# GpSimd takes two of the four normalisations of each step in the second node stage of a graph network

## The reference

```python
def _layernorm(x, axis=-1, eps=1e-05):
    m = jnp.mean(x, axis=axis, keepdims=True)
    v = jnp.var(x, axis=axis, keepdims=True)
    return (x - m) / jnp.sqrt(v + eps)
...
    x = _layernorm(x + _L0_gnn_ref(x, edge_index, L0_gnn_W1, L0_gnn_b1, L0_gnn_W2, L0_gnn_b2), axis=-1)
    x = _layernorm(x + _L1_gnn_ref(x, node_vec1, src, dst, edge_attr_4, ...), axis=-1)
```

## Time and profile before

| | |
|---|---|
| time, median of 3 executions | 7610.92 us (7610.32 to 7613.86) |
| the profiled execution, its own time | 7614.77 us |
| its span in the trace | 7612.9 us |
| mean granted clock of TensorE | 0.872 of full speed |
| busy share of the span: PE, VectorE, ACT, GpSimd | 87%, 62%, 45%, 64% |
| second node stage: first load issued to the edge stage's first load issued | 3411.7 to 3529.1 us from the span's start |
| edge stage, from then on | 4083 us |

### The profile page before, as it was taken

One profiled execution on the slowest core, in us unless ns is written; L12 is line 12 of the kernel. 1 busy time (PEld: TensorE's weight loads), 2 busy tenths in 40 slices (PEclk: granted clock), 3 DMA queues, 4 the chain that ended last, 5 costly groups with the idle time before them and its releaser, 6 DMA issues.

```text
span 7612.9 us, 125645 instructions
## 1 busy us (share of the span) xinstructions
PE 6617.5 (87%) x37688; PEld 5566.4 (73%) x37689; DVE 4748.7 (62%) x9176; ACT 3399.5 (45%) x6948; POOL 4890.6 (64%) x4864
## 2 busy tenths in 40 slices
PE   6899987999987999986888888888888888888887
PEld 4666656888876888875777777777777777777776
DVE  9999984333334333337666666666666666666665
ACT  5999974555545555543222222222222222222322
POOL 2211103777774777774777777777777777777775
PEclk9999999999999999998777777777777778787876
DMA  3666556555545555544223333233233333333331
GB/s 81 131 133 131 125 121 188 162 167 167 166 136 167 166 167 167 167 140 138 83 85 85 84 84 85 84 85 85 84 85 84 84 85 84 84 85 84 85 84 55
DMA packets 604288, 868.26 MB, mean 114 GB/s; under 512 B 217478, under 2 KB 470461, under 8 KB 599025
## 3 DMA queue, kind: packets, MB, share of 16 engines
q0 software_dynamic: 158000, 437.63, 22.0%
q1 hardware_dynamic: 419980, 414.21, 19.2%
q10 hardware_dynamic: 26036, 12.80, 0.6%
HBM read 706.91 MB, written 157.30 MB: 114 GB/s over the span
## 4 chain that ended last, share of the span: by engine, by line
POOL 34%; issue 13%; DMA 3%; DVE 2%; POOLq 1%; DVEq 0%; SPq 0%; PE 0%; ACT 0%; ACTq 0%
POOL t_rows L1758 34%; DMA t_rows<-table,t_ends 2%; DMA t_attrs<-in_edge_attr 1%; DVE t_msg_ad L2022 1%; POOLq L179 0%; DVE t_msg_bc L2036 0%; DVE t_cg L2021 0%; SPq L1730 0%; DVE t_msg_ad L2024 0%; POOLq L1756 0%; DVE t_ge L2018 0%; DVE t_rel L2109 0%; DVE acc L1999 0%; DVE t_msg_bc L2031 0%; DVEq L2120 0%
## 5 line engine op out<-in xcount | busy, mean ns | idle before, releaser
L1758 POOL DMA_INDIRECT t_rows<-table,t_ends x3224 | 3048.0, 945 | 1005.5 <-issue 967.7
L1035 POOL DMA_INDIRECT c_early<-table,c_first_src x1408 | 1559.0, 1107 | 661.3 <-issue 452.7
L1937 PEld LDWEIGHTS t_sums<-t_hot,t_msg_ad 128*128 128x128 f32 x6464 | 952.0, 232 | 922.5 <-issue 921.6
L1779 ACT ACTIVATE t_weight<-t_weight,t_attrs 128x64 f32<-128x64 f32 x3224 | 691.9, 302 | 2092.1 <-PE t_weight L1880 2084.0
L1125 ACT ACTIVATE c_wide_act<-c_raw 128x1024 fp32r<-128x1024 uint8 (+1 forms) x1120 | 1160.0, 1039 | 880.1 <-PE c_sums L1269 876.7
L1937 PE MATMUL t_sums<-t_hot,t_msg_ad 128*128 x6464 | 986.5, 318 | 619.7 <-DVE t_hot L2116 618.2
L1204 DVE CAST c_wide_dve<-c_raw 128x1024 fp32r<-128x1024 uint8 (+1 forms) x1120 | 653.2, 585 | 1257.1 <-PE c_sums L1269 1256.2
L1269 PE MATMUL c_sums<-c_wide_act,c_parts 128*128 128x512 f32 (+1 forms) x4480 | 1213.3, 394 | 72.8 <-DVE c_parts L1188 62.3
L2018 DVE TENSOR_TENSOR t_ge<-t_rows,t_edge 128x768 f32<-128x768 f32 x403 | 384.7, 955 | 1207.3 <-DMA t_rows<-table,t_ends 1196.2
L1940 PE MATMUL t_sums<-t_hot,t_msg_bc 128*128 x6464 | 1090.3, 341 | 0.0
L1940 PEld LDWEIGHTS t_sums<-t_hot,t_msg_bc 128*128 128x128 f32 x6464 | 1054.3, 255 | 0.0
(11 more groups left out here) (240 smaller groups left out, 6778.9 us busy)
## 6 DMA issues: line engine op xcount, KB each, us to landing
c_raw<-a_dram SPq DMA_DIRECT2D x532, 448.0 KB, 3.5
a_dram<-a_a_sb POOLq DMA_DIRECT2D x39, 3136.0 KB, 18.2
t_scal<-in_edge_attr SPq DMA_DIRECT2D x403, 256.0 KB
t_rows<-table,t_ends POOLq DMA_INDIRECT x3224
c_early<-table,c_first_src POOLq DMA_INDIRECT x1408, 3.1
t_ends<-in_edges SPq DMA_DIRECT2D x403, 8.0 KB
t_attrs<-in_edge_attr SPq DMA_DIRECT2D x403, 16.0 KB
c_raw<-a_dram SPq DMA_DIRECT2D x28, 224.0 KB, 2.6
```

What stands on the lines that cost most here:

```text
L1035: pool.indirect_dma_start(out=rows_of_group[:, q % 2, t], out_offset=None, in_=table_of_rows, in_offset=bass.IndirectOffsetOnAxis(ap=c.fir ...
L1758: pool.indirect_dma_start(out=rows[:, slot, t, :], out_offset=None, in_=table, in_offset=bass.IndirectOffsetOnAxis(ap=ends[:, slot, t:t + ...
L1779: mul = act.activation(ad, ad, ACT.Copy, scale=attrs[:, slot, t, 0:1])
L1937: pe.matmul(sums[:, of, 0:WIDE], msg_ad[:, slot % 2, t, :], hot[:, of, t, :], start=t == 0, stop=t == T - 1)
```

## The change

In each step GpSimd normalises the upper half of the blocks (two of four; one of two in the last step) and VectorE the lower half. GpSimd's list becomes `[add_bias, normalise]`: in round i the bias of step i, then its share of the normalisation of step i-1. A new semaphore `x1_more` counts GpSimd's halves; whoever waited for `x1_ready` now waits for both (SP's store, PE's transposition, VectorE's residual two steps on).

```diff
-    def apply(self, dve, y, out, i, b, blocks):
-        dve.wait_ge(self.rstd_ready, i + 1)
-        for j, n in enumerate(blocks):
-            last = dve.tensor_scalar(out[0:n, j], y[0:n, j], self.mean_var[0:n, b, j, 0:1], self.rstd[0:n, b, j:j + 1],
+    def apply(self, engine, y, out, b, blocks, some):
+        for j in some:
+            n = blocks[j]
+            last = engine.tensor_scalar(out[0:n, j], y[0:n, j], self.mean_var[0:n, b, j, 0:1], self.rstd[0:n, b, j:j + 1],
                                      ALU.subtract, ALU.mult)
...
                     sp.wait_ge(x1_ready, i + 1)
+                    sp.wait_ge(x1_more, i + 1)
...
                     pe.wait_ge(x1_ready, i + 1)
+                    pe.wait_ge(x1_more, i + 1)
...
-                staged_steps(pool, [add_bias], AHEAD)
+
+                def normalise(i, slot, blocks):
+                    b = slot % 2
+                    due = worked_out(pool, rstd_reg, i + 1)
+                    if later(i, 2):
+                        turned_due = worked_out(pool, turned_reg, i - 1)
+                        stored_due = worked_out(pool, stored_reg, (i - b) * 8)
+                        pool.wait_ge(s.set_up, 1)
+                        pool.wait_ge(turned_ready, turned_due)
+                        pool.wait_ge(x1_stored[b], stored_due)
+                    pool.wait_ge(s.rstd_ready, due)
+                    s.apply(pool, y[:, b], x1[:, b], b, blocks, range(len(blocks) // 2, len(blocks))
+                            ).then_inc(x1_more, 1)
...
+                staged_steps(pool, [add_bias, normalise], AHEAD)
...
                         dve.wait_ge(x1_ready, i - 1)
+                        dve.wait_ge(x1_more, i - 1)
...
-                    s.apply(dve, y[:, b], x1[:, b], i, b, blocks).then_inc(x1_ready, 1)
+                    dve.wait_ge(s.rstd_ready, i + 1)
+                    s.apply(dve, y[:, b], x1[:, b], b, blocks, range(len(blocks) // 2)).then_inc(x1_ready, 1)
```

More of the change, by code:

```diff
@@ L1467, in second_nodes @@
         s.semaphores(sem)
+        x1_more = sem("x1_more")
         landed = [sem(f"landed{i}") for i in range(AHEAD)]
@@ L1573, in add_bias @@
                     last.then_inc(xb_ready, 1)
-                staged_steps(pool, [add_bias], AHEAD)
+                def normalise(i, slot, blocks):
[10 more added lines that the diff above has]
+                            ).then_inc(x1_more, 1)
+                rstd_reg, turned_reg, stored_reg = [pool.alloc_register(f"n2_pool_{n}") for n in
+                                                    ("rstd", "turned", "stored")]
+                staged_steps(pool, [add_bias, normalise], AHEAD)
             @block.vector
```

## The result

| | before | changed |
|---|---|---|
| median, 6 executions each | 7611.55 us (7610.12 to 7620.05) | 7647.89 us (7642.82 to 7657.89) |
| ratio | | 1.0049, 95% interval 1.0039 to 1.0060 |
| span of the profiled execution | 7612.9 us | 7641.0 us |
| node stage, first load issued to the edge stage's first load issued | 3411.7 to 3529.1: 117.4 us | 3402.3 to 3557.3: 155.0 us |

The kernel is 36 us slower, where +19 was forecast with +33 as the far end of the range. The stage grew by 37.6 us.

What follows compares the result with a forecast made beforehand. The node stage leaned on VectorE; the change puts GpSimd's normalisations and bias into its loop, 5.13 us a step against 4.27: 18.9 us plus 0.5 for the last round, +19.4, giving 7630 us, range 7626 to 7635, wider 7617 to 7644.

Steps and rivals of the forecast that it cites:

- the far end of the range: Node stage: two GpSimd instructions of 0.45 us plus both of VectorE's waited out, 1.58 us, +32.7 us, 7644.
- the lead: Node stage before the change: GpSimd adds the bias more than a step ahead of the VectorE residual that reads it.
- two normalisations on GpSimd: Link of the node-stage loop: GpSimd's two blocks take 0.80 us a step, bounds 0.50 and 0.90.
- What VectorE's normalisations cost GpSimd: Link of the node-stage loop: delay from VectorE's two normalisations starting on the same signal, 0.20 us, bounds nothing and 0.68.
- The casts beside gathers: Convolution rows used as guide: a 0.95 us gather takes 1.39 beside a 0.69 us cast, so 0.64 of it is added.
- The hand-overs: Semaphore links in the node-stage loop: 0.08 us to GpSimd and 0.10 us to VectorE.
- the last round: Node stage's final step, two blocks: 2.97 us before, forecast 3.46, adding 0.5 us.
- the drain: Transposition, features and stores behind the node stage's last round, claimed to keep their length.
- w: GpSimd's whole normalisation time per step, forecast 1.00 us; the total change is 19.4 + 23 x (w - 1.00).
- GpSimd is quick: Rival: GpSimd's two blocks run at the iota's pace, undisturbed by VectorE; 0.50 us, +7.9 us, 7619; chance 0.32.
- the lead survives: Rival: bias not behind the normalisation, PE's loop sets the step at 4.05 us; 5 us faster, 7606; chance 0.03.
- The engines block each other: Rival: GpSimd's and VectorE's normalisations exclude each other, 1.20 us or more a step, up to +32.7 us, 7644; chance 0.17.

## Why the prediction was wrong

**The mechanism was right.** GpSimd's list puts the bias behind the normalisation, the lead is lost, and the two stand in VectorE's loop. The run with the bias ahead gave 25 us back, the one with one block 17.

**The term that failed is "two normalisations on GpSimd", 0.80 us.** From the first's start to the bias it measured 1.54 us alone and 1.58 in the changed kernel, hence 1.49 and 1.53 without the gap of 0.05. I took one instruction for L1316 with fewer inputs, and as bound from above the add of two tensors, 0.452 us, on the thought that one tensor and two pointers can't cost more than two tensors. They can: 0.79. The pointers cost 0.18 us, a column 2.8 ns and not 1.67. With the 0.05 to the bias, the forecast's 0.80 + 0.20 + 0.05 = 1.05 became 1.58. The prediction had named this sign of a wrong size, an L1437 on GpSimd far from 0.4 us.

**"What VectorE's normalisations cost GpSimd", 0.20 us, was 0.04**: 1.58 us for the pair beside them, 1.54 alone. The 0.16 too many took back a part of the first error, by luck. With it stood the rule of the Trainium skill, "SBUF — State Buffer", section "SBUF: two separate sides", that a VectorE instruction in a two-port mode and a GpSimd instruction shut each other out for the whole instruction. The trace agrees for another pair: the add of the bias, which reads two tensors, holds up VectorE's normalisations until it ends (2.10 us for 1.12). For GpSimd's own normalisation beside VectorE's it does not, and the measurement decides: VectorE's pair took 0.66 us where 0.34 + 0.26 = 0.60 was its own, beside 1.61 us of GpSimd. The casts beside gathers were thus no guide to this pair. In the changed kernel the pair is over (3488.25) before the add begins (3489.26), so that other stop costs it nothing.

**The hand-overs were too short**: 0.08 and 0.10 us from rows of before, 0.20 to 0.21 and, in the two steps shown, 0.14 and 0.30 in the changed kernel. I read the first from an add with fewer waits ahead of it and the second from the stage's first step, outside the loop. Why they are longer was not tried. VectorE's normalisations start 0.11 us after the reciprocal and GpSimd's 0.20, so VectorE's were first, where I had GpSimd's first.

The other links held: bias 1.27, residual to reciprocal 2.64. The sum of measured links is 0.205 + 1.58 + 1.27 + 0.22 + 2.64 = 5.92 us, and the two steps shown take (3499.30 - 3487.48) / 2 = 5.91 from the first reciprocal's end to the third's. Normalisations 0 and 22 lie at 3411.64 and 3540.74:

```profile
3411.64 0.66 DVE L1437 TENSOR_SCALAR n_x<-n_y,n_mean_var,n_rstd 128x128 f32<-128x128 f32 x2
...
3540.74 0.66 DVE L1437 TENSOR_SCALAR n_x<-n_y,n_mean_var,n_rstd 128x128 f32<-128x128 f32 x2
```

That is 129.1 us or 5.87 a step, 35.2 more than before. The remaining 2.4 lie behind it: the last round takes 4.28 us (reciprocals at 3540.49 and 3544.77) where it took 2.97, 1.3 more and not 0.5, and the drain, which was to keep its length, is 1.1 longer.

In the forecast's own formula, 19.4 + 23 x (1.53 - 1.00) = 31.6 us; the hand-overs add 23 x (0.205 + 0.22 - 0.18) = 5.6, together 37.2, beside the 37.6 measured. The far end of the range, w = 1.58, came near the true 1.53 only by adding to two instructions of 0.45 two delays of 0.34 that did not occur. That was luck, and the hand-overs took the time past it.

**The rivals.** "GpSimd is quick" and "the lead survives" did not come. The run with the bias ahead gave the second its condition, and it was 12.4 us slower where the rival had 5 us faster: the rival left out that the residual waits for GpSimd's half even so. "The engines block each other" was nearest in time but not in cause: what VectorE's normalisations cost GpSimd's was 0.04 us a step.

## What to carry to other kernels

Before giving an engine with idle time a second job, look at how far it runs ahead: work that it did a step early becomes late when it is queued behind something that waits for the present step. A price for an instruction that the trace doesn't show is bounded by rows with the same kind of operands, and pointers to numbers per partition are operands too. Relieving the busiest engine of a step pays only down to the next loop; here one block moved, with the bias ahead, left 0.3 us in the whole stage.

## What the runs showed of the hardware that was not expected

- A GpSimd `tensor_scalar` with two pointers on 128 columns takes 0.79 us from start to start, a `tensor_tensor` of 128 columns 0.45; minus a mean and times a scale for 256 columns takes 1.38 us as two `tensor_tensor` with broadcast inputs and 1.58 as two `tensor_scalar`.
- GpSimd's add of two tensors holds up VectorE's `tensor_scalar` beside it until it ends: four take 2.10 us instead of 1.12. It does not hold up VectorE's statistics, which took 0.87 us beside the add and 0.87 in the changed kernel (at 3491.90), where no add lies beside them, nor its residual, 1.12 us beside the add and without it.
- What GpSimd's normalisation costs VectorE's pair beside it went with its form: 0.60 us with one operation and one pointer, 0.66 with two pointers, 0.80 with constants, 1.01 with two `tensor_tensor`. Why was not tried.
